# Shorter statistics instructions on the vector engine, and a new instruction order, in a fused attention and feed-forward layer

## The reference, cut to what matters

```
x  = x + layer_xattn(layernorm(x))            # C = 4 channels, H = 256
  qkv_in = rat_read(h, W, gamma, beta, 3)     # y = einsum('blhc,hoc->bloh'); normalise each of 3 outputs over 256
  attn   = causal attention with rope, 16 heads of 16
  h      = rat_write(h, attn, ...)            # h * A + out * B, with softplus, exp and a division
  mlp_in = rat_read(h, ..., 2)                # the same with 2 outputs
  h      = rat_write(h, silu(gate) * up, ...) # gate and up: context weights, 1024 wide
x  = x + ffn(layernorm(x))                    # 1024 -> 3584 -> 1024, gated with silu
  each ffn weight is  base + mean(|w - base|) * sign(w - base),  for w1, w3 and w2
```

## Time and profile before

| | |
|---|---|
| median of 3 runs | 1392.75 us (1390.5 to 1395.87) |
| the profiled execution | 1392.75 us |
| its span, first to last instruction | 1390.8 us |
| busy PE, DVE, ACT, POOL | 1279.0, 831.0, 527.5, 388.3 us |
| first matmul of the closing gate sequence on PE | at 459.61 us |
| mean granted PE clock | 0.965 of full speed |

### The profile page before, as it was taken

The page is one execution under the profiler, slowest core; times in us unless marked ns, Lnnn a source line. Parts: engine busy times, 40 slices in busy tenths (PEclk is TensorE's granted clock), DMA queues, the critical chain, the costliest instruction groups (busy, mean ns, idle before and its releaser), DMA issues.

```text
span 1390.8 us, 16812 instructions
## 1 busy us (share of the span) xinstructions
PE 1279.0 (92%) x6548; PEld 1010.8 (73%) x6548; DVE 831.0 (60%) x1174; ACT 527.5 (38%) x813; POOL 388.3 (28%) x206
## 2 busy tenths in 40 slices
PE   4778777898897898999999999999999999999998
PEld 3545454556575786888888888888888888888887
DVE  5668776878678635636464555545463736364555
ACT  3567665675565454222222222221313222222220
POOL 1112424143334566222222222222222222222210
PEclk9899988999898899999999999999999999999999
DMA  8166767773421585222223222232222222222212
GB/s 343 42 238 235 274 242 257 273 290 134 181 91 63 194 318 196 110 102 92 91 91 111 100 93 91 91 117 96 91 91 91 102 104 97 91 91 104 98 41 121
DMA packets 53826, 197.55 MB, mean 142 GB/s; under 512 B 6626, under 2 KB 6900, under 8 KB 53236
## 3 DMA queue, kind: packets, MB, share of 16 engines
q1 hardware_dynamic: 53748, 196.49, 38.6%
HBM read 192.27 MB, written 4.19 MB: 141 GB/s over the span
## 4 chain that ended last, share of the span: by engine, by line
PE 75%; DVE 10%; ACT 5%; DMA 4%; issue 3%; POOL 2%; SPq 1%; DVEq 0%; ACTq 0%
PE pair L1009 40%; PE quad L1031 22%; DVE negwide L1444 2%; PE quad L955 2%; DMA late<-in_mean_w 2%; PE pair L992 2%; PE quad L945 1%; PE pair L883 1%; POOL late L1722 1%; ACT prob L1174 1%; DMA part<-in_mean_w 1%; PE pair L864 1%; PE pair L898 1%; PE quad L992 1%; DVE part L1625 1%
## 5 line engine op out<-in xcount | busy, mean ns | idle before, releaser
L1727 POOL TENSOR_TENSOR raw_w<-raw_w,raw_base 128x1024 f32<-128x1024 f32 x84 | 214.4, 2554 | 618.3 <-DMA raw_base<-in_mean_w 618.2
L1009 PE MATMUL pair<-xnT_hi,w_hi 128*128 128x512 f32 x880 | 344.8, 392 | 1.3 <-DVE xnT_lo L1635 1.3
L1009 PE MATMUL pair<-xnT_hi,w_lo 128*128 128x512 f32 x880 | 343.9, 391 | 0.0
L1009 PE MATMUL pair<-xnT_lo,w_hi 128*128 128x512 f32 x880 | 343.8, 391 | 0.0
L1245 ACT ACTIVATE w_hi<-raw_w 128x1024 fp32r<-128x1024 f32 x84 | 88.9, 1059 | 509.8 <-DVE raw_w L1531 509.6
L1681 DVE TENSOR_TENSOR work<-sgf,pair 128x512 f32<-128x512 f32 x56 | 38.5, 687 | 289.4 <-PE pair L1009 289.4
L1009 PEld LDWEIGHTS pair<-xnT_hi,w_hi 128*128 128x128 f32 x880 | 166.3, 189 | 36.7 <-DVE xnT_lo L1635 1.4
L1009 PEld LDWEIGHTS pair<-xnT_hi,w_lo 128*128 128x128 f32 x880 | 166.3, 189 | 34.6
L1009 PEld LDWEIGHTS pair<-xnT_lo,w_hi 128*128 128x128 f32 x880 | 166.2, 189 | 34.7
L1649 DVE TENSOR_TENSOR hid<-hid,quad 128x512 f32<-128x512 f32 x208 | 139.2, 683 | 66.2 <-PE quad L1031 66.2
L1531 DVE SCALAR_TENSOR_TENSOR raw_w<-raw_w,coeff,raw_base 128x1024 f32<-128x1024 f32 x84 | 155.7, 1855 | 10.6 <-ACT raw_w L1227 10.1
(11 more groups left out here) (236 smaller groups left out, 1590.3 us busy)
## 6 DMA issues: line engine op xcount, KB each, us to landing
raw_w<-in_w SPq DMA_DIRECT2D x84, 512.0 KB, 3.6
raw_base<-in_mean_w SPq DMA_DIRECT2D x84, 512.0 KB, 4.5
ctxw<-in_w SPq DMA_DIRECT2D x28, 512.0 KB, 4.8
ctxw<-in_mean_w SPq DMA_DIRECT2D x28, 512.0 KB, 6.6
part<-in_w SPq DMA_DIRECT2D x24, 512.0 KB, 4.2
part<-in_mean_w SPq DMA_DIRECT2D x24, 512.0 KB, 5.5
big<-in_w SPq DMA_DIRECT2D x18, 512.0 KB, 4.4
big<-in_mean_w SPq DMA_DIRECT2D x18, 512.0 KB, 6.2
```

What stands on the lines that cost most here:

```text
L1009: a = pe.matmul(banks[gate_bank(u, b)], ww[:, k, :], xx[:, k, :], start=k == 0 and n == 0, stop=k == KF - 1 and n == 2)
L1727: pool.tensor_tensor(w[:, :], w[:, :], base[:, :], ALU.subtract).then_inc(f_diff, 1)
```

## The change

The three helpers that compute on the small statistics tiles are rewritten. `shift_rows` uses one `scalar_tensor_tensor` in place of one `tensor_scalar`, so that mean and factor are both tensor inputs. `shift_reads` uses one `scalar_tensor_tensor` of three or two columns in place of three or two `tensor_scalar` of one. `spread_reads` adds eps to all variances at once, in place of one instruction for each output. The table `WORK` gets new durations for these steps, and the third number for most of them. `weight` takes the durations without `SLOW`. `FIRST`, `AHEAD`, `SLOW`, `PULL` and `MEASURE_WEIGHT` get new values; so the planner makes another order for all of phase one.

```diff
--- before.py
+++ after.py
@@ -115,17 +115,17 @@
 RAT = [("PE", 1.48), ("DVE", 0.27), ("PE", 0.27), ("ACT", 0.26), ("PE", 0.59), ("ACT", 1.48), ("DVE", 1.52, 0.2),
        ("ACT", 0.83), ("DVE", 2.68, 0.25), ("POOL", 1.81), ("POOL", 0.72), ("DVE", 1.94, 1.94)]
 WORK = {
-    "front": [("DVE", 1.71), ("POOL", 0.55), ("DVE", 0.15), ("ACT", 1.24), ("PE", 1.04), ("ACT", 1.02), ("PE", 1.92),
-              ("DVE", 1.76), ("POOL", 0.86), ("DVE", 0.28), ("ACT", 1.48), ("PE", 0.83), ("ACT", 2.19),
+    "front": [("DVE", 1.71), ("POOL", 0.55), ("DVE", 0.15, 0.15), ("ACT", 1.24), ("PE", 1.04), ("ACT", 1.02), ("PE", 1.92),
+              ("DVE", 1.64, 0.2), ("POOL", 0.86), ("DVE", 0.16, 0.16), ("ACT", 1.48), ("PE", 0.83), ("ACT", 2.19),
               ("PE", 2.76), ("DVE", 2.4, 0.7), ("PE", 1.04), ("ACT", 1.08)],
     "turnmax": [("PE", 0.39), ("DVE", 0.42)],
     "out": [("ACT", 0.38)],
     "row": [("PE", 0.61), ("DVE", 0.72), ("PE", 0.39), ("ACT", 0.38)],
-    "back": RAT + [("PE", 1.04), ("DVE", 1.21), ("PE", 1.91), ("DVE", 1.31), ("POOL", 0.7), ("DVE", 0.22),
+    "back": RAT + [("PE", 1.04), ("DVE", 1.21), ("PE", 1.91), ("DVE", 1.25, 0.2), ("POOL", 0.7), ("DVE", 0.16, 0.16),
                    ("ACT", 1.02), ("PE", 0.61), ("ACT", 1.51)],
     "mlp": [("PE", 1.89), ("ACT", 0.38), ("DVE", 0.42)],
     "finish": [("PE", 5.32)] + RAT[1:8] + [("DVE", 3.55, 1.25)] + RAT[9:] + [("SP", 1.65), ("POOL", 0.73), ("DVE", 1.71),
-                                                                           ("POOL", 0.55), ("DVE", 0.15)],
+                                                                           ("POOL", 0.55), ("DVE", 0.16, 0.16)],
     "measure": [("SP", 3.3), ("POOL", 2.35), ("ACT", 1.25)],
     "x": [("SP", 1.65)],
     "ctx": [("SP", 6.6)],
@@ -380,7 +380,7 @@
             missing = [y for y in users[x] if y not in weight]
             todo += missing
             if not missing:
-                weight[x] = engine_and_time(x)[1] + HOP + max([weight[y] for y in users[x]], default=0.0)
+                weight[x] = found_work(*x)[1] + HOP + max([weight[y] for y in users[x]], default=0.0)
                 todo.pop()
     for n in range(SOON):
         for part in range(3):
@@ -488,22 +488,22 @@
 
 
 
-MEASURE_WEIGHT, PULL = 3.684, 0.02239
-FIRST = {"back": (-7.6, -8.8, -9, -8.9), "coef": (5.8,), "ctx": (2.7,), "diag": (18.6, 20.6), "early": (-8.1,),
-         "fill": (3.3, -0.3, -1.6, -1), "finish": (-1.6, -2.4, -2.9, -11.7), "front": (-3.8, -4.3, -4.8, -6),
-         "measure": (-0.3,), "mlp": (1.7, -0.6, -0, -0.3), "norm": (0.3, -7.1, 7.2, -7.5),
-         "out": (0.8, 3.2, -3.3, -1.6), "prep": (-0.6,), "raw": (-20,), "row": (1.3, 3.1, 2.7, -0.5),
-         "turnmax": (3.3, 0.9, -0.8, 0.3), "use": (-1.7, -1.6, 0, -3.1), "weigh": (2.4, 0.9, -0.2, -0.6), "x": (-3.3,)}
+MEASURE_WEIGHT, PULL = 3.413, 0.02268
+FIRST = {"back": (-7.6, -8.6, -9, -8.4), "coef": (4.2,), "ctx": (8.8,), "diag": (21.4, 16.2), "early": (-10.8,),
+         "fill": (4.7, 0.3, -1.3, -1.4), "finish": (-1.7, -2.4, -3.3, -8), "front": (-3.1, -3.7, -4.7, -6.1),
+         "measure": (-0.4,), "mlp": (3.7, -2.1, 2.3, 0.8), "norm": (8, 5.6, -1.6, 2.2), "out": (8.9, 8.3, 6.5, 6.2),
+         "prep": (0.2,), "raw": (-11.8,), "row": (12.6, 7.9, 1.1, 2.5), "turnmax": (5.1, 1.1, -0.6, -1.1),
+         "use": (-1.3, -1.9, 0.2, -3.1), "weigh": (3, 0.7, -0.8, -1), "x": (3.9,)}
 AHEAD = {
-         "back": (7.8, 91.4, 7.5, 15.6, 9.4, 8.2, 37.2, 8, 7, 3, 5.3, 16.5, 6.8, 57.5, 7.4, 43.8, 7.3, 15.1, 56.5, 5.8, 33.1),
-         "coef": (3.7, 4.2, -14.3), "ctx": (4.1,), "diag": (-15.8,), "early": (-0.7, -1, 2.6, -11.3), "fill": (0.6,),
-         "finish": (-1, 3.6, 1.2, 4.2, 8.7, 5.7, 1.8, 2.4, 3.5, -3.3, 6.9, 1.3, 7.8, -4.9, 2.5, -7.6, 6.7),
-         "front": (4.5, 5.8, 7.1, 4, 5.3, 5.6, 5.2, 6.5, 5.8, 15.9, 6.2, 6.3, 5, 5.2, 5.9, 4.9, 5),
-         "measure": (2.3, 0.4, -0.1), "mlp": (-4.7, 0.3, 10.6), "norm": (-2.3, -11.6, 9.1, 5.8), "out": (3.6,),
-         "prep": (-2.8, 3.1, -8.7), "raw": (0.9, 9.1, 8.8), "row": (6.4, -0.1, -0.1, -1), "turnmax": (-0.5, 4.2),
-         "use": (2.1,), "weigh": (-1.8,), "x": (13.2,)}
+         "back": (7.7, 29.4, 10.5, 21.8, 8.4, 7.7, 16.4, 7.7, 7.7, 2.8, 6.4, 9.3, 6.7, 25, 7.2, 18.7, 7.3, 12, 13.3, 5.9, 8),
+         "coef": (-1.5, -2.8, -9.6), "ctx": (7.7,), "diag": (-17.6,), "early": (-4.9, 6.4, -0.2, 4.3),
+         "finish": (-0.5, 5.1, 2.6, 0.6, 6.9, 1.2, 1.1, 2.3, 6.5, -0.8, 4.8, 4.3, 3.6, -0.4, 3.8, 6.4, 2.7),
+         "front": (5.6, 3.6, 22.9, 3.5, 5.8, 5.5, 8.3, 6.1, 5.1, 21.1, 29.3, 5.7, 4.9, 4.9, 5.5, 4.8, 5.9),
+         "measure": (3.8, 0.6, -0.1), "mlp": (-6.4, 3, 7.3), "norm": (-2.9, -11.3, -2.7, -4.1), "out": (2.8,),
+         "prep": (-3, -3.5, -3.8), "raw": (2.1, 8.3, 8.1), "row": (0.6, -2, 4.6, 1.6), "turnmax": (-0.6, 7.8),
+         "use": (2,), "weigh": (-1.5,), "x": (3.5,)}
 OWN = {}
-SLOW = {"PE": 1.048, "DVE": 1.096, "ACT": 1.157, "POOL": 1.098}
+SLOW = {"PE": 1.107, "DVE": 1.101, "ACT": 1.135, "POOL": 1.135}
 
 NAMES = ("w1", "w3", "w2")
 GROUP = 2
@@ -1375,13 +1375,11 @@
 
             def shift_rows(st, done):
 
-                dve.tensor_scalar(st[:, 14:15], st[:, 12:13], st[:, 15:16], -1.0, ALU.mult, ALU.mult).then_inc(done, 1)
+                dve.scalar_tensor_tensor(st[:, 14:15], st[:, 12:13], -1.0, st[:, 15:16], ALU.mult, ALU.mult).then_inc(done, 1)
 
             def shift_reads(st, ways, done):
-                for o in range(ways):
-                    a = dve.tensor_scalar(st[:, ways + o:ways + o + 1], st[:, 18 + 2 * o:19 + 2 * o], st[:, o:o + 1], -1.0,
-                                          ALU.mult, ALU.mult)
-                a.then_inc(done, 1)
+                mean = st[:, 18:18 + 2 * ways].rearrange("p (o two) -> p two o", two=2)[:, 0, :]
+                dve.scalar_tensor_tensor(st[:, ways:2 * ways], mean, -1.0, st[:, 0:ways], ALU.mult, ALU.mult).then_inc(done, 1)
 
             def spread_reads(found, st, done):
 
@@ -1393,9 +1391,8 @@
                 for o in range(ways):
                     a = dve.bn_aggr(st[:, 18 + 2 * o:20 + 2 * o], st[:, 6 * o:6 * o + 6])
                 chained(a)
-                for o in range(ways):
-                    a = dve.tensor_scalar(st[:, o:o + 1], st[:, 19 + 2 * o:20 + 2 * o], EPS, None, ALU.add)
-                a.then_inc(done, 1)
+                var = st[:, 18:18 + 2 * ways].rearrange("p (o two) -> p two o", two=2)[:, 1, :]
+                dve.tensor_scalar(st[:, 0:ways], var, EPS, None, ALU.add).then_inc(done, 1)
 
             def front(t, part):
                 if part == 0:
```

## The result

The changed kernel takes 1406.59 us (median of 7 runs, 1396.32 to 1411.62), against 1390.5 for the kernel before (7 runs, 1384.19 to 1395.87). The ratio is 1.0108 [1.0064, 1.0152]: it is slower, by about 1%. Two later measurements of the same file gave 1.009 [1.0052, 1.0129] and 1.0104 [1.0072, 1.0137]. I had predicted 1389.5, with a range of 1377 to 1402 and 0.22 for slower.

A forecast was written before the change was run, and what follows sets the result against it. It took the end as matmul-bound on PE and the phase ahead of the closing gate matmuls as steps waiting for each other, no engine full. 1392.75 - 2.5 + 1.5 - 2 = 1389.75, said as 1389.5, range 1377 to 1402.

The forecast's parts named there:

- The new order: I take -2 us: Phase one in the new planned order: other waits, buffer turns and load times, priced by no row, taken as 2 us gained.
- ±12: Bound on the new order's effect either way: a tenth of DVE's idle time ahead of the closing gate sequence, 12 us.
- order that is worse for other reasons: Rival: the new order of phase one loses time for reasons other than POOL holds, 1400 to 1405 us; chance 0.07.
- the direct saving of 2.5: Shorter statistics instructions on the chain: five front tiles at 0.41 and two back ones at 0.22 us, between 0 and 5.7.
- 9.3: Holds by POOL, in us, beyond which the forecast range up to 1402 was said to leave cases out.
- +1.5 for holds: New shifts and eps instructions waiting for POOL: nine old places, 12.6 us in all, 1.5 us taken on the path.
- At 48.47: A shift held 2.3 us by POOL, where L1625 was already held by the same instruction; DVE itself loses 0.2 us.
- the cover of PE's early gate work: Last shift, at 470.77: PE still has early gate matmuls, so its 2.3 us hold costs nothing; without cover, 2.3.
- my open case: Whether POOL holds the two- or three-column eps instruction: no row decided, so it was counted as held.
- G + 931.2: Time as the start G of the closing gate sequence, 459.6 us, plus 81.8 and 849.4; the change acts only on G.
- 849.4: Matmul-only stretch from 541.42 us to the end, PE busy 845.5 us, which the change can't shorten.
- The stretch of 81.8 us: From the first closing gate matmul at 459.61 us to 541.4 us, with no edited line on the chain.

The follow-up runs named there:

- order_alone: The changed kernel with the three old helpers, so the new order with the old instructions: 1402.59 us, 1.0087 of the kernel before.
- after_third: The changed kernel unchanged, run again as the reference for the kernels with extra matmuls in PE's pauses: 1402.62 us, 1.0104 of the kernel before.
- instr_second: The kernel before with the three new helpers and its old order, measured a second time: 1386.26 us, 0.9965 of the kernel before.
- old_fit: The changed kernel with MEASURE_WEIGHT, PULL, FIRST, AHEAD and SLOW of the kernel before: 1452.05 us, 1.0456 of the kernel before.
- the leads: Planner leads on eight PE steps of the second MLP block: +6 and +10 in the changed kernel, 1439.5 and 1444.86 us; -10 in `instr_alone`, 1414.87 us.
- instr_alone: The kernel before with the three new helpers, its planner numbers and order kept: 1386.94 us, 0.997 of the kernel before.
- holds_alone: The kernel before with its 56 shifts still one by one, each as an instruction with two tensor inputs: 1388.26 us, 1.0006 of the kernel before.
- eps_alone: The kernel before with only `spread_reads` changed, eps added for all outputs at once: 1389.73 us, 0.9999 of the kernel before.
- after_again: The changed kernel unchanged, run again as the reference beside the split of the change: 1398.67 us, 1.009 of the kernel before.
- after_gap: The changed kernel with 180 extra identity matmuls ahead of 21 steps before which PE had idled for over 1 us: 1403.7 us, 1.0108 of the kernel before.
- The late block: Second MLP block (tiles 8 to 15), reaching PE at 343.75 us in the changed kernel, 335.1 before; moved by planner leads: 1439.5, 1444.86 and 1414.87 us.
- the fillers: Extra identity matmuls that compute nothing, put into PE's pauses: 1403.7 us in the changed kernel with 180, 1395.57 in `instr_alone` with 157.

## Why the prediction was wrong

**The failed step is "The new order: I take -2 us".** It measured about +12 with the old instructions (`order_alone`, 1.0087), and 16 with the new ones (`after_third` against `instr_second`). I had no row for it, and took a sign from what the planner knows ("the new plan knows the holds of POOL and the shorter steps"). `old_fit` and the leads show how little that carries: the order answered to small edits with 28 to 62 us, far outside of my ±12. My bound came from DVE's idle time that could be closed. An order can also make the work itself slower, which no idle time bounds, and that is what the profiles show: equal idle time on PE, and the same matmuls 5.7 us longer. The "order that is worse for other reasons" was in the text, at 0.07 and at 1400 to 1405. That was the outcome, with a mean of 1402.3 over all executions (the first median, 1406.59, is above even that), and its chance was too low, since nothing spoke for the gaining side except the argument just named. The end of the range was also reasoned a little short: with the direct saving of 2.5, 1402 stands for holds of 11.8 us, and not for 9.3.

**The direct saving was right in the old order, with its net a little small.** I summed -2.5 for shorter instructions and +1.5 for holds, -1.0. `instr_alone` gives -4.2 and -4.9 us on the ratios (0.997 and 0.9965), with intervals of ±3.5 and ±3.1. In the new order no saving shows: the changed kernel's mean is 1402.3, that of `order_alone` 1401.9. The durations: the shift measured 0.15 to 0.16, I had taken 0.17; eps measured 0.169, I had taken 0.155. The one-column form with two tensor inputs is 0.15 against the 0.206 it replaces, so even `shift_rows` gains 0.05 and not 0.036 us a piece.

**The holds came as described, and are not the main loss.** They appear in all kernels with the new shifts, at most 2.35 us, as the rows on POOL foretold. At 48.47 I had said that the hold replaces one that L1625 had already; after, the shift takes 2.30 on the chain and L1622 behind it takes 1.21 in place of 2.90: so it was. For the last shift I took the cover of PE's early gate work. In the changed kernel the cover is gone: 1.86 us lie on the chain (475.18), and the gate matmuls behind it take 2.2 us longer at the lower clock. I had priced that case at 2.3 and left out the clock. `holds_alone` has the hold on its chain too, but without the slower gate sequence (5.74 us):

```profile
468.01 2.36 DVE x_stat L1378
```

and is still at 1.0006, so in the old order my 1.5 us for the holds were not too few. The eps instruction was my open case, and I had counted it as held. It was, in both forms: with two columns 1.54 us in `eps_alone` and 1.44 in the changed kernel, with three 0.67 in `after_again` and 2.36 in `after_gap`. The one-column tensor_scalar was never held, with 0.216 us at most in all traces. The Trainium skill (VectorE: DVE Perf Modes, section Mode 2×_2P — use both read ports for one tensor) lets a one-input instruction in SBUF split its outermost dimension in halves and read one half through each port, if that dimension is even, or odd and equal for source and destination. One column leaves nothing to split, and two and three columns meet the condition; the traces agree for all three widths.

**G + 931.2 was right in its large part only.** The 849.4 is 849.0. The stretch of 81.8 us lost its start: the chain no longer runs over PE's stock of early gate work but through DVE's last block, so the term G has no row in the new chain. The later gate sequence moved from 481.12 to 481.83 in this profile and to 485.12 in `after_again`, and from there to the sum it took 61.7 us in place of 59.5. What I had written as a sign that the forecast is wrong ("if the stretch behind G changes, for instance because other pieces of the early gate work are left for it") took place.

**What stays open.** That the order costs the 12 us is shown. The profiles show 5.7 us of it, in the time that the same matmuls take, with the same idle time on PE; for the rest there is no trace. Why this order does so is not shown. Measured are a PE with less to do from 330 to 345 us, a chain that ends in DVE's last block, two held shifts of 1.6 and 1.9 us late on the chain (`instr_second` has one of 2.0), and more time at the lower clock. The late block got no support, but was never tested alone. The held shifts are excluded as the main cause by `order_alone`; that they eat the gain of the instructions in the new order is possible and not shown. The clock goes with 8.8 of the 12 us, and a higher clock does shorten the kernel's matmuls; that it alone makes the difference between the two orders is not shown, since the fillers were too long for their pauses. Which pauses of the new order bring the clock down is open too.

**The better version.** The old order with the new instructions, `instr_alone`, beats both kernels: 0.997 [0.9945, 0.9995] and 0.9965 [0.9943, 0.9987] of the kernel before, some 4 us, and 16 us below the changed one (12 in the first group of runs).

## What to carry to other kernels

Where an edit of instructions also changes the numbers of a planner, measure the two apart: here the instructions gained 4 us in the old order and nothing in the new one, and the order that came with them lost 12. An order with fitted numbers can lose much more by a small change of its inputs (28 to 62 us here) than the change was to gain, and a forecast for a new one should be nearly even between the signs and wide, unless a row shows it. When single executions differ by 1%, compare many of them, and read a pair of profiles only for where and not for how much. Split the time ahead of the point that decides into busy and idle: equal idle time and longer busy time point to slower work, and not to more waits.

## What the runs showed of the hardware

- The spread of one kernel's executions goes with the granted clock: r = -0.86 over 88 executions, 0.95 us less per 0.001 more.
- The same 24 gate matmuls took 5.77 us at a granted clock of 1.00, with PE busy 10.13 of the 11.10 us before them, and 7.98 us at 0.70, after PE had been busy 1.09 of 4.80 us.
- A one-column instruction with two tensor inputs takes 0.15 us where the tensor_scalar with a pointer operand takes 0.206 and the one with an immediate 0.154. It is held by POOL up to 2.35 us, and the tensor_scalar of one column never was (0.216 us at most). The 128x2 and the 128x3 tensor_scalar were held, for up to 2.26 and 2.36 us in place of 0.17.
- 180 matmuls of 128x128 in PE's pauses raised the granted clock ahead of the sum from 0.92 to 0.95 and shortened the kernel's own matmuls by about 22 us. They took 48 us of PE themselves, 0.26 each, and the kernel gained nothing.
